# Layer-0 attention: powers of both heads squared by quadrants, the off-diagonal block computed a stage ahead, turned powers evicted by two engines

## The reference

```python
mixed = silu(conv(hidden_states @ w_qkv))      # four taps along the tokens
q, k, v = split(mixed)                         # 16, 16 and 32 heads of 128
q, k = l2norm(q) * DK ** -0.5, l2norm(k)
def step(Sm, inp):                             # for each token
    q_, k_, v_, g_, b_ = inp
    Sm = Sm * exp(g_)
    kv = einsum('bhk,bhkv->bhv', k_, Sm)
    delta = (v_ - kv) * b_
    Sm = Sm + einsum('bhk,bhv->bhkv', k_, delta)
    return Sm, einsum('bhk,bhkv->bhv', q_, Sm)
og = o * silu(z)
return (og * rsqrt(mean(og * og) + EPS) * norm_w) @ w_out
```

## Time and profile before

| | before |
|---|---|
| median of three runs | 6041.1 us |
| profiled execution, span | 6046.2 us |
| TensorE busy | 5221.5 us (86%) |
| VectorE busy | 3480.2 us (58%) |
| ScalarE busy | 3055.8 us (51%) |
| GpSimd busy | 1178.3 us (19%) |
| DMA | 103.57 MB, 17 GB/s in the mean |

### The profile page before, as it was taken

The page is one execution under the profiler, slowest core; times in us unless marked ns, Lnnn a source line. Parts: engine busy times, 40 slices in busy tenths (PEclk is TensorE's granted clock), DMA queues, the critical chain, the costliest instruction groups (busy, mean ns, idle before and its releaser), DMA issues. The chain is left out here.

```text
span 6046.2 us, 91895 instructions
## 1 busy us (share of the span) xinstructions
PE 5221.5 (86%) x32318; PEld 3893.8 (64%) x32318; DVE 3480.2 (58%) x6531; ACT 3055.8 (51%) x8923; POOL 1178.3 (19%) x1352
## 2 busy tenths in 40 slices
PE   5799999999989999989999699899998597399969
PEld 4477777877877778877887555555555354255545
DVE  3466666676666667666766566555552554543331
ACT  2466666666656666666666344344441244325421
POOL 0222222322222222222232100011110321002210
PEclk7799999999999999999999799899999798688879
DMA  2000000000000000000000100100000100000000
GB/s 85 19 19 17 13 19 19 18 17 17 19 19 13 17 19 19 17 14 19 22 19 13 46 1 1 65 1 0 0 0 20 27 1 13 21 1 1 1 21 14
DMA packets 51094, 103.57 MB, mean 17 GB/s; under 512 B 12848, under 2 KB 20176, under 8 KB 49520
## 3 DMA queue, kind: packets, MB, share of 16 engines
q1 hardware_dynamic: 50672, 98.07, 5.4%
HBM read 90.43 MB, written 5.52 MB: 16 GB/s over the span
## 5 line engine op out<-in xcount | busy, mean ns | idle before, releaser
L896 ACT ACTIVATE dh_pb<-bank 64x128 f32<-64x128 f32 x3072 | 831.4, 271 | 272.5 <-PE bank L670 239.3
L684 PE MATMUL bank<-dh_cw,dh_pb 128*128 128x128 f32 x5120 | 701.5, 281 | 113.0 <-ACT dh_pb L896 111.4
L684 PEld LDWEIGHTS bank<-dh_cw,dh_pb 128*128 128x128 f32 x5120 | 635.5, 193 | 191.1 <-ACT dh_pb L896 164.4
L1034 DVE SCALAR_TENSOR_TENSOR dh_kq<-bank,dh_conv_kq,dh_kq 128x511 f32<-128x511 f32 (+2 forms) x408 | 305.4, 749 | 184.8 <-ACT dh_kq L853 173.6
L902 ACT ACTIVATE dh_cw<-bank 128x256 f32<-128x256 f32 x640 | 244.9, 385 | 255.1 <-PE bank L684 247.9
L621 PE MATMUL bank<-hT,dh_w_kq 128*128 128x512 f32 x544 | 276.7, 633 | 83.2 <-DVE dh_kq L1034 75.3
L1034 DVE SCALAR_TENSOR_TENSOR dh_v<-bank,dh_conv_v,dh_v 128x511 f32<-128x511 f32 (+2 forms) x384 | 284.2, 747 | 91.3 <-ACT dh_v L853 82.2
L1797 PE MATMUL bank<-moe_h_split,moe_w 128*128 128x512 bf16 x1200 | 277.1, 381 | 14.6 <-PEq L89 14.6
L633 PE MATMUL bank<-dh_w_vz,hT 128*128 128x256 f32 x1024 | 245.5, 383 | 22.0 <-ACT dh_zs L864 22.0
L1128 DVE TENSOR_TENSOR dh_zz<-dh_zz,bank 128x512 f32<-128x512 f32 x130 | 89.2, 686 | 283.0 <-PE bank L597 281.1
L621 PE MATMUL bank<-hT,dh_w_vz 128*128 128x512 f32 x512 | 242.5, 596 | 8.6 <-DVE dh_v L1034 8.6
(11 more groups left out here) (416 smaller groups left out, 12170.8 us busy)
## 6 DMA issues: line engine op xcount, KB each, us to landing
dh_rates<-delta_rates SPq DMA_DIRECT2D x130, 256.0 KB, 3.6
dh_w_vz<-in_L_wvz SPq DMA_DIRECT2D x17, 512.0 KB, 3.3
mod_w<-in_L_wmod SPq DMA_DIRECT2D x4, 1536.0 KB, 7.0
dh_w_kq<-in_L_wkq SPq DMA_DIRECT2D x18, 256.0 KB, 2.6
dh_wo<-in_L_wo SPq DMA_DIRECT2D x16, 256.0 KB, 4.2
moe_w<-in_L_w13T SPq DMA_DIRECT2D x1, 3200.0 KB, 15.7
later_gates<-mod_gate SPq DMA_DIRECT2D x3, 1024.0 KB, 4.0
gate<-later_gates SPq DMA_DIRECT2D x6, 512.0 KB, 3.4
```

The costliest lines, as they stand in the source:

```text
L684: last = pe.matmul(square(j)[:, b, :, :], pb[j][:, b, :], src[:, :, b, :], start=True, stop=True)
L896: last = act.activation(out[half, :, o, half], src[halves[o], :, half], ACT.Copy)
L1034: dve.scalar_tensor_tensor(y, pj_bank(n)[:, 0:S - i], taps(n)[:, TAPS - 1 - i:TAPS - i], y, ALU.mult, ALU.add).then_inc(s["v_cs" if i < TA ...
```

## The change

Both heads are handled together by each instruction, in tiles whose order is (kind of pair of sequences, head, sequence in the pair). The powers are squared as 64x64 matmuls: 16 matmuls a power, each with 64 rows and 64 columns of the array and 128 moving columns (64 for the last power). For one kind of sequence the result stays on its half of the partitions, for the other it crosses to the other half and back with each squaring. The two kinds have a bank each, the halves of one kind share it. The turned power needs no block diagonal tile: it is evicted as four instructions of 64x256, two by ScalarE (`power`, lower partitions) and two by VectorE (`power_second`, upper partitions).

`power_u` copies the power of both heads in one instruction, `grow` adds the product in one or three. `w_prod`, `x_prod`, `zeta` and `w_copy` go. In their place the off-diagonal block of the full inverse is made once a stage, one chunk ahead: `turn_first` (transposes of the first block), `first_copy`, `off_first`, `off_copy`, `off_second`, `corner_copy` into the corner of `ttb`. `z_prod` then applies the whole inverse. The lists of the stages are written anew, with the projections and the like in numbered slots (`tensor_fill`, `scalar_fill`, `vector_fill`), which hold the same work as before; `normed` stands behind `decay`, `start_power` and `qk_mask`. `off_diagonal` on GpSimd waits for `off_first` of the stage before. `squares` waits for `t_wo` and `y_copy` also waits for it.

```diff
-        self.bank = [ctx.enter_context(nc.psum_tensor(f"bank{i}", [P, 512], F32)) for i in range(8)]
+        bank = lambda i, shape: ctx.enter_context(nc.psum_tensor(f"bank{i}", shape, F32))
+        first, self.pair = bank(0, [P, 512]), bank(1, [P, 2, 512])
+        self.bank = [first, self.pair[:, 0, :], self.pair[:, 1, :], *(bank(i, [P, 512]) for i in range(3, 8))]
...
+    def across(kind, half):
+
+        return halves[half if kind == 0 else 1 - half]
...
+    def square_power(pe, t, i):
         if i:
-            pe.wait_ge(h["v_c"], 5 * t + i)
+            pe.wait_ge(s["v_w"], (POWERS - 1) * t + i)
         else:
-            after(pe, h["v_ttb"], t)
-        src = cw[j] if i else c0[j]
-        for b in range(NB):
-            last = pe.matmul(square(j)[:, b, :, :], pb[j][:, b, :], src[:, :, b, :], start=True, stop=True)
-        last.then_inc(h["t_ct"], 1)
+            after(pe, s["v_td"], t)
+        for e in range(2):
+            pe.wait_ge(s["v_pt" if e else "a_pt"], POWERS * t + i + 1)
+            for j in HEADS:
+                at = 2 * (2 * j + e) * HALF
+                for kind in range(KINDS):
+                    for half in range(2):
+                        width = HALF if i == POWERS - 1 else 2 * HALF
+                        last = pe.matmul(bank[1 + kind][across(kind, half), at:at + width], pt[halves[half], kind, j, e, :],
+                                         moving(i, halves[half], kind, j, e), start=True, stop=True)
+        last.then_inc(s["t_sq"], 1)
...
+    def off_first(pe, t):
+        pe.wait_ge(s["a_t1"], t + 1)
+        for j in HEADS: pe.wait_ge(hs[j]["p_nt"], t + 1)
+        for j in HEADS:
+            for g in range(2):
+                for o in range(2):
+                    last = pe.matmul(turn_at(4 + 2 * j + g)[halves[1 - o], :], off[0:HALF, j, 2 * g + o, :],
+                                     pt[0:HALF, j, g, o, :], start=True, stop=True)
+        last.then_inc(s["t_yo"], 1)
...
+    def power(act, t, i):
+        act.wait_ge(s["t_tr"], POWERS * t + i + 1)
+        after(act, s["t_sq"], POWERS * t + i)
+        if i == 0:
+            after(act, s["t_zo"], t)
+        for half in range(2):
+            last = act.activation(pt[halves[half], :, :, 0, :].rearrange("p k j n -> p (k j) n"),
+                                  turned_half(0, half), ACT.Copy)
+        last.then_inc(s["a_pt"], 1)
+
+    def power_u(act, t, i):
+        act.wait_ge(s["t_sq"], POWERS * t + i + 1)
+        act.activation(both(cw[:, :, :, 1, :, :]), both(pair[:, :, :, :, place(i, True), :]), ACT.Copy).then_inc(s["a_u"], 1)
...
+    def grow(dve, t, i):
+        dve.wait_ge(s["a_u"], (POWERS - 1) * t + i + 1)
+        after(dve, s["v_w"], (POWERS - 1) * t + i)
...
+    def power_second(dve, t, i):
+        dve.wait_ge(s["t_tr"], POWERS * t + i + 1)
+        after(dve, s["t_sq"], POWERS * t + i)
+        if i == 0:
+            after(dve, s["t_zo"], t)
+        for half in range(2):
+            last = dve.tensor_copy(pt[halves[half], :, :, 1, :].rearrange("p k j n -> p (k j) n"), turned_half(1, half))
+        last.then_inc(s["v_pt"], 1)
...
+        turn_power(pe, t, 0)
+        tensor_fill(pe, q, a, 0)
+        v_turn(pe, t, 0)
+        if old:
+            for j in HEADS: ks(pe, t, j)
+        square_power(pe, t, 0)
+        v_turn(pe, t, 1)
+        tensor_fill(pe, q, a, 1)
+        turn_power(pe, t, 1)
+        tensor_fill(pe, q, a, 2)
+        z_prod(pe, t, 0)
+        square_power(pe, t, 1)
+        z_prod(pe, t, 1)
...
+        qk_prod(pe, t)
+        tensor_fill(pe, q, a, 8)
+        square_power(pe, t, 5)
+        y_turn(pe, t, 0)
+        turn_first(pe, t)
+        y_turn(pe, t, 1)
+        tensor_fill(pe, q, a, 9)
+        off_first(pe, t)
+        w_out(pe, t, 0)
+        off_second(pe, t)
+        w_out(pe, t, 1)
+        tensor_fill(pe, q, a, 10)
...
+        power(act, t, 0)
+        v_scaled(act, t, 0)
+        scalar_fill(act, q, a, 0)
+        power_u(act, t, 0)
+        v_scaled(act, t, 1)
+        scalar_fill(act, q, a, 1)
+        power(act, t, 1)
...
+        power_second(dve, t, 0)
         if old:
             for j in HEADS: rhs(dve, t, j)
...
+        vector_fill(dve, q, a, 0)
+        grow(dve, t, 0)
+        power_second(dve, t, 1)
+        vector_fill(dve, q, a, 1)
...
+        grow(dve, t, 4)
+        power_second(dve, t, 5)
         if a: state(dve, t, 1)
...
         kk_mask(dve, t)
-        for j in HEADS: normed(dve, t, j)
-        for j in HEADS: grow(dve, t, 5, j)
+        vector_fill(dve, q, a, 7)
+        for j in HEADS: decay(dve, t, j)
+        start_power(dve, t)
         qk_mask(dve, t)
-        for j in HEADS: decay(dve, t, j)
-        for j in HEADS: start_power(dve, t, j)
-        inverse(dve, t, 0)
+        normed(dve, t, 0)
+        vector_fill(dve, q, a, 8)
+        inverse(dve, t)
+        normed(dve, t, 1)
+        vector_fill(dve, q, a, 9)
         collect(dve, t)
-        inverse(dve, t, 1)
...
-        pool.wait_ge(h["t_w"], t + 1)
+        after(pool, s["t_yo"], t)
```

More of the change, by code:

```diff
@@ L660, in qk_prod, with turn_power @@
         each(pe, B_AUX, lambda b: key(par, c, b), lambda b: query(par, c, b)).then_inc(s["t_qk"], 1)
-    def turn_power(pe, t, i, j):
-        h = hs[j]
+    def turn_power(pe, t, i):
         if i:
-            pe.wait_ge(h["a_c"], 5 * t + i)
+            pe.wait_ge(s["a_u"], (POWERS - 1) * t + i)
         else:
-            after(pe, h["v_u"], t)
-        src = cw[j] if i else c0[j]
[L669 to L673, removed]
@@ L687, in v_turn, with off_second @@
+    def off_second(pe, t):
+        pe.wait_ge(s["a_yo"], t + 1)
+        for j in HEADS:
+            for g in range(2):
+                for o in range(2):
+                    last = pe.matmul(turn_at(2 * j + g)[halves[o], :], pt[HALF:P, j, g, o, :],
+                                     ttb[HALF:P, j, 2 * g + o, HALF:P], start=True, stop=True)
+        last.then_inc(s["t_zo"], 1)
     def v_turn(pe, t, j):
@@ L926, in y_copy @@
         act.wait_ge(hs[j]["t_yt"], t + 1)
+        after(act, s["t_wo"], t)
         if a > 1:
@@ L1088, in decay, with start_power @@
             .then_inc(h["v_et"], 1)
[L1090 to L1092 removed]
+    def start_power(dve, t):
         dve.wait_ge(s["v_kk"], order(t) + 1)
[L1094 to L1105 removed]
@@ L1107, in inverse @@
-    def inverse(dve, t, j):
-        h = hs[j]
-        dve.wait_ge(h["t_ct"], 6 * t + 6)
-        dve.wait_ge(h["v_c"], 5 * t + 5)
-        dve.wait_ge(h["t_x"], t + 1)
-        for half in halves:
-            last = dve.tensor_tensor(ttb[j][half, :, half], cw[j][half, 1, :, :], square(j)[half, :, 1, :], ALU.add)
-        last.then_inc(h["v_ttb"], 1)
+        after(dve, s["t_sq"], POWERS * t + 1)
+        for j in HEADS:
+            dve.wait_ge(hs[j]["v_et"], order(t) + 1)
+            for half in halves:
+                split = lambda v: v[half, :, half].rearrange("p (k e) n -> p k e n", k=KINDS)
+                last = dve.tensor_tensor(c0[half, :, j, 0, :, :], split(kkm), split(et[j]), ALU.mult)
@@ new lines, in inverse @@
+    def inverse(dve, t):
+        dve.wait_ge(s["t_sq"], POWERS * (t + 1))
+        dve.wait_ge(s["v_w"], (POWERS - 1) * (t + 1))
+        for j in HEADS: dve.wait_ge(hs[j]["t_z"], t + 1)
+        after(dve, s["t_zo"], t)
+        for half in range(2):
+            for kind in range(KINDS):
+                out = ttb[halves[half], :, 2 * kind:2 * kind + 2, halves[half]]
+                last = dve.tensor_tensor(out, cw[across(kind, half), kind, :, 0, :, :], pair[halves[half], kind, :, :, 0, :],
+                                         ALU.add)
+        last.then_inc(s["v_td"], 1)
@@ L1470, in _ @@
             for j in HEADS: v_turn(pe, 0, j)
-            for f in (ks, z_prod, w_prod, x_prod, qs, pu, y_turn):
+            for f in (ks, z_prod, qs, pu, y_turn):
                 for j in HEADS: f(pe, 0, j)
@@ L1481, in _ @@
         def _(dve):
-            for f in (rhs, zeta, q_state, output, normed):
+            for f in (rhs, q_state, output, normed):
                 for j in HEADS: f(dve, 0, j)
```

571 lines of the change are left out of this document (294 added, 277 removed).

## The result

The changed kernel takes 6405.2 us in the median of four runs (6402.32 to 6412.53). The kernel before takes 6037.85 us in the four runs beside it (6032.09 to 6044.46). The ratio is 1.0605, with a 95% interval from 1.059 to 1.062: 6% slower, 367 us. The forecast was 6117 us, 76 above the time before, with a range that ended at 6360: slower was right, by how much was not.

What follows compares the result with a forecast made beforehand. TensorE bounded the kernel before; afterwards the order of TensorE's and VectorE's queues would. 193.2 us plus 7.6 for the clock gives 200.8 a pair, 4.8 more; 16 pairs add 76 to 6041: 6117 us, own range 6040 to 6220, wider 5930 to 6360.

Steps and rivals of the forecast that it cites:

- The signs: In the profile after: TensorE busy below 82%, clock below 0.96, VectorE about 37 us a stage, a=1 near 45, a=2 above 50.
- Rival 2: Busy time of TensorE or VectorE at 92% sets each stage: 166 us a pair, 5560 us, halfway 5800; chance 0.13.
- the ladder: Step-by-step timing of a head pair's four stages through the queues waiting for each other: 193.2 us against 196.0 before.
- clock term: Lower TensorE clock in the stage's tail behind the hole ahead of y_turn: 1.9 us a stage, 7.6 a pair.
- clock bounds: Between no clock fall and two a stage, around the one assumed; given as the forecast's own range, 6040 to 6220 us.
- no fall: No lower clock in the stage's tail: 193.2 us a pair, 5996 us; as a rival, chance 0.20.
- The squaring: Squaring a power on TensorE as 32 quadrant instructions running side by side: 1.0 us, bounds 0.9 to 3.6.
- rival 4: No quadrants run at once in the squarings: 2.6 us more each, 52 a pair, 6950 us; chance 0.05.
- rival 3: Row halves sharing one bank run in turn, squaring 1.8 us: 12.8 us a pair more, 6320 us; chance 0.17.
- VectorE terms: VectorE durations in the powers and stage end: eviction pair 0.75 us, start_power 2.7, inverse four overlapping additions of 0.417.
- two falls: Upper bound for the lower clock: two such stretches a stage instead of the one of 1.9 us.
- `normed`'s move: VectorE's normed goes behind decay and start_power, so y_turn, w_out and the new block wait; no separate size.

Runs made afterwards that it cites:

- experiment 7: Changed kernel with grow's three additions made one 128x512 instruction in powers 1 to 4, part of the inverse then wrong: 6262.43 us.
- 9: Changed kernel with idle TensorE products ahead of y_turn, ahead of qk_prod and, in a=2, ahead of the second squaring: 6338.01 us.
- experiment 10: Changed kernel with idle TensorE products a stage, two ahead of y_turn and three ahead of qk_prod: 6356.77 us.
- 6: Changed kernel with ScalarE evicting all turned powers, normed and inverse ahead of decay and start_power, and two idle products ahead of y_turn: 5890.1 us.
- 2: Changed kernel with VectorE's normed and inverse moved ahead of decay and start_power: 6185.01 us.
- Experiment 3: Changed kernel with two idle 512-column TensorE products a stage between the last squaring and y_turn: 6298.34 us.
- experiment 4: Kernel before the change, with VectorE's normed moved behind decay, start_power and qk_mask: 6529.72 us.
- 5: Changed kernel with ScalarE evicting all turned powers, and normed and inverse ahead of decay and start_power: 5921.42 us.

## Why the direction was right and the size wrong

**The picture held.** TensorE's work fell, and two queues that wait for each other in turn took the gain away and more. The signs that the prediction named came, some of them only nearly: TensorE busy 82% from 300 to 3100 us (2298 of 2800; below 82 was named), clock 0.85, VectorE 39 us a stage (37 was named), idle time put down to kk_mask, `normed` and `inverse`; a=1 at 48.4 us (near 45 was named), a=2 at 59.5. Rival 2 (resources set the stage) fell: the ladder is what set it.

**How much of the direction was luck.** The forecast was slower by its clock term alone: the ladder without it, 193.2 us a pair, lay below the 196.0 of before. Both turned out too short, so the direction did not hang on that term in the end: less the 11.6 us that the lower clock cost in the tail (worked out below), the pair's 218.3 would still be 206.7. And the forecast's own range, 6040 to 6220, is not what its clock bounds give: no fall gives 5996, two give 6239.

**The squaring was right.** 32 instructions took 1.10 us in most bursts. The groups from 300 to 3500 us (busy, mean ns, idle ahead):

```profile
L718 PE MATMUL bank<-dh_cw,dh_pt 64*64 64x128 f32 (+1 forms) x9408 | 337.2, 281 | 71.7 <-DVE dh_cw L1199 46.2 <-DVE dh_pt L1227 7.6 <-DVE dh_cw L1206 7.0
L1227 DVE COPY dh_pt<-bank 64x256 f32<-64x256 f32 x704 | 300.4, 427 | 103.8 <-PE bank L702 89.4
```

337.2 us for 9408 are 1.15 for 32, lower clock and the half-width ones included; forecast 1.0. In a burst at full clock four instructions start within 0.02 us (at 1231.39), and the next four 0.11 behind them. Four quadrants run side by side, so rival 4 falls. So does rival 3, although its time, 6320, lies nearer to the result than the forecast: each half of the rows writes its own partitions of one bank, and they don't wait for each other. The rule of the Trainium skill (TensorEngine Tiling (Array Packing), "Gotcha 1: PSUM Pressure") that different row tiles cannot access the same bank at once is not borne out here: by it a squaring would have been 1.8 us.

**The ladder was right in its steps and short in its VectorE terms.** In a=2 the forecast and the trace, from the first turn on: first squaring ends 5.6 and 5.6 us, convolution 10.2 and 10.4, second `power_second` 11.5 and 11.9, third 15.2 and 16.9, kk_mask 33.45 and 36.9, inverse 43.05 and 47.1, end 52.9 and 59.3. All stages, up to the end of kk_mask: 38.9, 30.3, 37.0 and 30.0 (from VectorE's order of time: the start of kk_mask plus its 0.69, less the stage's first turn) against 35.5, 28.65, 33.45 and 27.8: 10.8 us more a pair. From there to `turn_first` 38.0 against 34.9: 3.1 more. Which terms:

- An eviction pair on VectorE takes 0.87 us, not the 0.75 that came from letting neighbours overlap; they don't at half the partitions. `grow` takes 1.28, not 1.07. Six times 0.12 and four times 0.2 are 1.5 us a stage, 6 a pair; at the 0.66 that experiment 7 shows up to kk_mask they make 4.
- The four additions of `inverse` take 1.71, not 1.4, for the same reason: 1.2 of the 3.1. `start_power` takes 3.24 in three stages and 1.69 in a=0, where the forecast had the mean of before, 2.7, throughout: 0.6 more a pair.
- `z_prod` and the products near it at the lower clock, which the prediction had only for the tail: 1.2 a pair by experiments 9 and 10, in a=2.
- The rest, some 7 us a pair (110 us in all), lies for the most part in the powers; no experiment took it apart.

**The clock term was mis-sized.** The prediction took one fall a stage at 1.9 us, 7.6 a pair. From `turn_first` to the next stage the pair took 10.76 + 9.70 + 12.22 + 11.47 = 44.15 us; the ladder had 32.95 for it without the clock: 11.2 more. The first four rows are these stretches of the changed kernel, a=0 to 3; the other four are the same stretches in stages where the clock was granted in full (a=0 in experiment 10, a=1 and a=2 in 6, a=3 in 2); columns as above:

```profile
1372.59:1383.35 10.76, 10.76 (x64) 7.22 (x65) 2.92 (x4) 4.43 (x9) 0.00 (x0) 0.71 0.01 2
1422.06:1431.76 9.70, 9.68 (x65) 6.32 (x65) 2.92 (x4) 4.42 (x9) 1.42 (x2) 0.82 0.01 2
1479.00:1491.22 12.22, 12.22 (x73) 8.47 (x74) 4.20 (x6) 3.90 (x8) 1.41 (x2) 0.77 0.13 33
1530.28:1541.75 11.47, 11.47 (x60) 8.77 (x61) 0.67 (x1) 2.82 (x7) 1.41 (x2) 0.50 0.01 1
...
1349.69:1357.70 8.01, 7.99 (x64) 5.74 (x65) 2.92 (x4) 4.44 (x9) 0.00 (x0) 1.00 0.00 0
...
1067.01:1074.94 7.93, 7.93 (x66) 5.75 (x66) 7.82 (x9) 4.50 (x9) 4.77 (x4) 1.00 0.23 68
1298.87:1308.51 9.64, 9.64 (x73) 7.25 (x73) 9.13 (x12) 4.50 (x9) 7.47 (x5) 1.00 0.06 10
...
433.29:440.29 7.00, 6.51 (x61) 4.95 (x61) 6.93 (x8) 2.70 (x6) 4.77 (x4) 1.00 0.42 109
```

At full clock the pair's tails are 32.6 us (0.5 of it a wait, in a=3), so the ladder's sizes were right here: `w_out` between quadrant products costs more than forecast (1.93 against 1.73), the off-diagonal products less (0.61 against 0.8). The lower clock costs 11.6 us a pair, 1.8 to 4.5 a stage, where 7.6 stood. The size came from a hole of 1.3 us, after which the level was back within 4.5 us; in a=3 here it lasted to the end of the stage. The bound "two falls", 15.2, would have covered the term, but not the result. Experiment 3 shows that it counts: at least 107 us.

**The sum.** 4.8 us a pair were forecast; 10.8 + 3.1 + (11.2 less 7.6) come on top: 22.3, as measured. Of 291 us missed (367 less 76), some 220 are the ladder up to `turn_first` and 58 the tail; the other dozen are not placed. So two steps failed: the ladder up to `turn_first`, of which VectorE's copies and additions on half the partitions, taken with an overlap that they don't have, are the largest part that is known and some 7 us a pair stay open; and the clock, taken as one short fall a stage.

**Cause and cure.** The prediction named `normed`'s move as a new wait, and gave it no price of its own. Experiments 2, 4 and 5 give it: 220 us in the changed kernel alone, 288 us once ScalarE evicts (6209.13 less 5921.42), and 490 us in the kernel before. VectorE's evictions are 196 us alone, 264 with the order mended (6185.01 less 5921.42). Neither the quadrants nor the off-diagonal block are at fault: with both corrected, the same products make a kernel 1.9% faster than before, and 3.2% with the tail in a better order.

## What to carry to other kernels

When two in-order queues hand work to each other, work taken from the one that was busiest gains only if what it waits for next is not pushed back: price each move in a queue by everything that it is moved behind, unless a row shows work that covers it (in experiment 4, 6.3 us of wait for a move of 7.7). Two corrections that each mend one of two waits in a row are worth more together than apart, so try them together before giving either up. And a hole on TensorE is paid twice where a stretch of TensorE alone follows it, by the hole and by the lower clock behind it; idle products that last up to the next real one were then cheaper than the hole. Ahead of `qk_prod`, where VectorE set the end of the next stretch too, they gave nothing back, and the clock fell behind the next hole instead.

## What the runs showed of the hardware

- Four 64x64 quadrants ran side by side with two row halves writing one bank on different partitions: 32 instructions of 128 columns in 1.10 us (1.15 in the mean), four starting within 0.02 us and the next four 0.11 later, where 16 of the full array take 1.95.
- The lower clock level stayed through 13 us of nearly gapless work in a=3 (granted clock 0.50, `w_out` 3.78 us against 1.99), much of it quadrant and transpose work; in a=2, with a projection in the same place, it had ended before `w_out`. What made the difference was not tried.
- VectorE's instructions on 64 partitions (0.42 us) follow one another without overlap, 0.85 to 0.87 a pair, while 512-wide ones of 128 partitions start 0.61 apart at a duration of 0.69.
- VectorE's multiplications of 64x256 in `start_power` took 1.17 to 1.20 us while GpSimd ran its 128x512 multiplication (L1386) and 0.42 else, in the kernel before (L1259) as well. What they share was not tried.
- A change between quadrant products and the full array costs TensorE about 0.1 us: eight instructions of 256 columns take 1.73 us from start to next start, 1.83 behind quadrant products and 1.93 between two groups of them.
- Added work made the kernel faster: four instructions a stage more, 107 us less, and 31 less in a kernel whose clock was at 0.96.
